# Counting the edges of each relation inside the attention instead of in the loop over edge chunks

## The reference, cut to what matters

```python
# layer 0: weighted sum over the edges
support = xn @ W
out = segment_sum(support[src] * edge_weight[:, None], dst, 625)
# layer 1: for each relation r the mean over the edges of that type
for r in range(8):
    mask = (edge_type == r)
    sums = segment_sum(xn[src] * mask[:, None], dst, n)
    cnt = segment_sum(mask, dst, n)
    out = out + (sums / max(cnt, 1)[:, None]) @ weight[r]
# layer 1 also: 16-head linear attention (exp features of 256 columns), added to x
```

## Time and profile before

| | us |
|---|---|
| median of 3 runs | 3110.17 (3106.64 to 3110.68) |
| the profiled execution | 3112.09 |
| its span in the trace | 3110.1 |
| PE busy | 2754.4 (89%) |
| DVE busy | 1789.7 (58%) |
| ACT busy | 1330.7 (43%) |
| POOL busy | 289.2 (9%) |
| mean granted TensorE clock | 0.948 of 2.4 GHz |

### The profile page before, as it was taken

One profiled execution on the slowest core, in us unless ns is written; L12 is line 12 of the kernel. 1 busy time (PEld: TensorE's weight loads), 2 busy tenths in 40 slices (PEclk: granted clock), 3 DMA queues, 4 the chain that ended last, 5 costly groups with the idle time before them and its releaser, 6 DMA issues.

```text
span 3110.1 us, 39323 instructions
## 1 busy us (share of the span) xinstructions
PE 2754.4 (89%) x16055; PEld 2433.4 (78%) x16055; DVE 1789.7 (58%) x2040; ACT 1330.7 (43%) x1761; POOL 289.2 (9%) x278
## 2 busy tenths in 40 slices
PE   3684666898999999999997599989999999999988
PEld 3674556687777777777765499978999999999987
DVE  5455883445788778877886355553344444444443
ACT  1324663224676676666772366641322222112221
POOL 3774331010000000000001000000000000000000
PEclk7796888999999999999998699999999999999999
DMA  4232003136899999999996411114222221123211
GB/s 132 56 88 61 1 1 82 63 89 237 313 327 329 316 328 329 329 321 335 324 331 176 158 36 42 42 50 133 84 65 59 65 65 59 55 80 109 75 59 67
DMA packets 129110, 456.59 MB, mean 147 GB/s; under 512 B 20503, under 2 KB 33175, under 8 KB 127795
## 3 DMA queue, kind: packets, MB, share of 16 engines
q1 hardware_dynamic: 98698, 389.85, 36.3%
q0 software_dynamic: 14512, 30.02, 4.3%
q10 hardware_dynamic: 15722, 34.22, 3.1%
HBM read 416.43 MB, written 37.49 MB: 146 GB/s over the span
## 4 chain that ended last, share of the span: by engine, by line
PE 69%; DVE 9%; DMA 7%; issue 5%; POOL 4%; ACT 3%; DVEq 1%; another core or an unknown queue 1%; ACTq 0%; SPq 0%; POOLq 0%
PE ps L188 68%; POOL scr_edges L908 4%; DMA er<-in_wd 3%; DVE es_l L213 2%; DMA wr<-in_root 1%; ACT es_h L640 1%; DMA scr_adj<-Aall 1%; DVE Aw L201 1%; DVE x L201 1%; DVE od L205 1%; DMA wr<-in_Wq 1%; DVE T_l L213 1%; POOL ws_l L213 1%; DVE st L729 1%
## 5 line engine op out<-in xcount | busy, mean ns | idle before, releaser
L213 DVE TENSOR_TENSOR es_l<-er,es_h 128x1408 fp32r<-128x1408 f32 (+1 forms) x455 | 653.1, 1445 | 192.1 <-ACT es_h L640 188.7
L640 ACT ACTIVATE es_h<-er 128x1408 fp32r<-128x1408 f32 (+1 forms) x455 | 563.4, 1242 | 270.1 <-PE ps L188 197.6
L640 ACT ACTIVATE ws_h<-wr 128x1024 fp32r<-128x1024 f32 (+1 forms) x181 | 190.9, 1056 | 591.3 <-PE ps L188 544.0
L188 PE MATMUL ps<-T_h,ws_h 128*128 128x314 f32 x1856 | 425.0, 310 | 18.3 <-DVE ws_l L213 13.4
L188 PE MATMUL ps<-T_h,ws_l 128*128 128x314 f32 x1856 | 422.2, 309 | 0.0
L188 PE MATMUL ps<-T_l,ws_h 128*128 128x314 f32 x1856 | 421.2, 309 | 0.0
L188 PEld LDWEIGHTS ps<-T_h,ws_h 128*128 128x128 f32 x1856 | 313.2, 191 | 21.4 <-issue 14.7
L213 DVE TENSOR_TENSOR ws_l<-wr,ws_h 128x1024 fp32r<-128x1024 f32 x165 | 200.4, 1216 | 200.1 <-ACT ws_h L640 197.5
L188 PEld LDWEIGHTS ps<-T_l,ws_h 128*128 128x128 f32 x1856 | 312.9, 191 | 0.0
L188 PEld LDWEIGHTS ps<-T_h,ws_l 128*128 128x128 f32 x1856 | 312.8, 191 | 0.0
L188 PE MATMUL ps<-es_h,xe_h 128*98 128x512 f32 (+1 forms) x768 | 207.9, 379 | 10.1 <-DVE es_l L213 7.1
(11 more groups left out here) (382 smaller groups left out, 5139.7 us busy)
## 6 DMA issues: line engine op xcount, KB each, us to landing
er<-in_wg SPq DMA_DIRECT2D x128, 704.0 KB, 6.7
er<-in_wu SPq DMA_DIRECT2D x128, 704.0 KB, 6.1
er<-in_wd SPq DMA_DIRECT2D x176, 512.0 KB, 5.0
wr<-in_rel SPq DMA_DIRECT2D x64, 512.0 KB
wr<-in_Wqkv SPq DMA_DIRECT2D x24, 512.0 KB
wr<-in_gate SPq DMA_DIRECT2D x16, 512.0 KB
wr<-in_w SPq DMA_DIRECT2D x14, 512.0 KB
scr_ei<-zrow ACTq DMA_DIRECT2D x1, 6272.0 KB, 30.1
```

The lines of the kernel that those rows point to most:

```text
L188: return e.matmul(out, l, r, start=start, stop=stop, skip_group_check=True)
L213: return e.tensor_tensor(lo, src, hi.bitcast(F32), ALU.subtract)
L640: q.e.activation(c.hi, c.at, ACT.Copy).then_inc(*self.s("high").up(c.key))
```

## The change

- The counts leave the loop over chunks, with the uint16 evictions, `Aall`, its three memsets and its store. The loop makes only the weights.
- The counts are made in the attention, and are there called tallies. `d_x` keeps x in memory meanwhile, since the tallies' buffers lie in x's place; x comes back after them.
- For each chunk POOL makes a one-hot `blc` (bf16), ACT makes `bod` = sign(n - target - 0.5) (bf16, "steps"), PE multiplies them (two matmuls of 314 columns), DVE adds the running sum of the bucket (`scalar_tensor_tensor` from PSUM into one of four `acc`), and POOL stores `acc` (0.314 MB) to the rows of its bucket by an indirect transfer, or to rows that nobody reads when the bucket goes on. Twice the counts are the differences of neighbouring columns.
- In each pair there are nine places (0 to 8) for two chunks: 0 after queries 0, 1 after the attend, 2 after projection 16+p, 3 after keys 1, 4 after the transposes, 5 after projection 9+p, 6 after queries 1, 7 after projection 1+p, 8 after values 1. The first are at place 4 of pair 0, the last at place 2 of pair 7.
- In the relations POOL loads twice the bytes for each relation (1.57 MB) and subtracts neighbouring columns (3135 elements a partition); ACT's ten copies at the start, and later five for each relation, are gone.
- `v_sort` has one instruction more before the indices and two elsewhere.

```diff
-        self.d_adj = nc.dram_tensor("scr_adj", (TP, NBK * NT), U16).ap()
+        self.d_adj = nc.dram_tensor("scr_adj", ((NBK + 1 + NCH) * TP, NT), F32).ap()
+        self.d_x = nc.dram_tensor("scr_x", (TP, T * D), F32).ap()
...
-        e.memset(m["Aall"].bitcast(I32)[0:TP, 0:5032], 0).then_inc(*self.s("zeros").up(0))
...
@@ t_adjacency
-            outs = self.t_pair(q, ("count", c))
-            for h in range(2):
-                ins = mm(e, outs[h][0:TP], lc[:, 0:TP], halves[h], True, True)
...
@@ a_adjacency
-                e.activation(two(u), ps.two(ps.group["count", c][0], slice(0, TP)), ACT.Copy).then_inc(*ps.out(("count", c)))
...
@@ v_adjacency
-                    e.reg_load(regs[G:G + n], m["off"][0:1, NCH + c:NCH + c + n])
...
-                o = m["Aall"][0:TP, bass.ds(v, NT)]
-                tt(e, o, m[f"c16{c % 2}"][0:TP, :], o, ALU.add).then_inc(*self.s("counts_added").up(c))
@@ p_adjacency
-        e.dma_start(self.d_adj, m["Aall"][0:TP, :]).then_inc(*self.landed("adjacency").up(0))
@@ a_spread, v_spread
-        q.wait_ge(self.landed("adjacency"), 0)
...
+    def tally(self, p, i):
+        n = 2 * (9 * p + i - 4)
+        return range(max(n, 0), min(n + 2, NCH))
+
+    def t_tally(self, q, p, i):
+        for c in self.tally(p, i):
+            outs = self.t_pair(q, ("tally", c))
+            q.wait_ge(self.s("chunk_sources"), c)
+            q.wait_ge(self.s("chunk_signs"), c)
+            for h in range(2):
+                ins = mm(q.e, outs[h][0:TP], m[f"blc{c % 4}"][:, 0:TP], m[f"bod{c % 4}"][:, h * H:(h + 1) * H], True, True)
+            ins.then_inc(*self.s("tallied").up(c))
+
+    def a_tally(self, q, p, i):
+        for c in self.tally(p, i + 1):
...
+            q.e.activation(m[f"bod{c % 4}"], self.iota, ACT.Sign, bias=m["bias"][:, c:c + 1]).then_inc(*self.s("chunk_signs").up(c))
+
+    def v_tally(self, q, p, i):
...
+            q.wait_ge(self.s("tallied"), c)
+            if c > 3:
+                q.wait_ge(self.landed(f"tally{c % 4}"), c - 4)
...
+                ins = stt(q.e, two(acc), two(was), m["same"][0:TP, c:c + 1], src, ALU.mult, ALU.add)
+
+    def p_attention(self, q):
+        q.wait_ge(self.s("normalized"), (2, T - 1))
+        e.dma_start(self.d_x, self.x).then_inc(*self.landed("x_kept").up(0))
...
+        for c in range(NCH + 2):
+            if c < NCH:
+                if c > 3:
+                    q.wait_ge(self.s("tallied"), c - 4)
+                e.tensor_scalar(m[f"blc{c % 4}"], self.iota[:, 0:128], seb[:, c, 0:1], None, ALU.is_equal).then_inc(*self.s("chunk_sources").up(c))
+            if c > 1:
+                c -= 2
+                q.wait_ge(*self.ps.done(("tally", c)))
...
+                e.indirect_dma_start(self.d_adj, to, m[f"acc{c % 4}"][0:TP, :], None).then_inc(*self.landed(f"tally{c % 4}").up(c))
...
+        e.dma_start(self.x, self.d_x).then_inc(*self.landed("x_back").up(0))
@@ v_attention (t_ and a_ alike; nine such lines in a pair)
             self.v_feature(q, "k", p, 0)
             self.v_feature(q, "q", p, 0)
+            self.v_tally(q, p, 0)
             if p:
                 self.v_tail(q, p - 1)
+            self.v_tally(q, p, 1)
             self.v_low(q, ("qkv", 16 + p))
+            self.v_tally(q, p, 2)
...
@@ p_relations
-            e.dma_start(m["A16"][0:TP, :], self.d_adj[:, r * T * NT:(r + 1) * T * NT]).then_inc(*self.landed("A16").up(r))
+            e.dma_start(steps, self.d_adj[r * N:(r + 1) * N, :].rearrange("(s p) n -> p s n", p=TP)).then_inc(*self.landed("steps").up(r))
+            q.wait_ge(self.landed("steps"), r)
+            if r > 1:
+                q.wait_ge(self.s("aggregated"), (("agg", r - 2), KD - 1))
+            e.tensor_tensor(rows(self.counts(r)[0:TP, :], T)[:, :, 0:NT - 1], steps[:, :, 1:NT], steps[:, :, 0:NT - 1], ALU.subtract).then_inc(*self.s("counts").up(r))
```

More of the change, by code:

```diff
@@ L249, in __init__ @@
         self.weights()
-        self.regs = [nc.alloc_register(mybir.EngineType.DVE, f"adj{i}") for i in range(16)]
+        self.regs = [nc.alloc_register(mybir.EngineType.DVE, f"adj{i}") for i in range(8)]
+        self.slots = [nc.alloc_register(mybir.EngineType.Pool, f"slot{i}") for i in range(8)]
     def memory(self, nc):
@@ L313, in memory @@
         at("st1", R2 + 13632, NBK * EC)
-        at("A16", R3, T * NT, U16)
-        at("ta0", R3 + 6304, NT)
-        at("ta1", R3 + 8832, NT)
-        at("icnt", R3 + 11360, NT)
+        at("dg", R2 + 13632, NCH + 1, F32R)
+        X = self.oX
+        for i in range(4):
+            at(f"bod{i}", X + i * 1280, NT, BF16)
+            at(f"blc{i}", X + 5120 + i * 256, 128, BF16)
+            at(f"acc{i}", X + 6144 + i * 2528, NT)
+        at("seb", X + 16256, NCH * 4)
+        at("bias", X + 18240, NCH)
+        at("same", X + 18752, NCH + 1)
+        at("bslot", X + 19264, NCH)
+        at("brows", X + 19776, NCH, I32)
+        at("steps", R3, T * NT)
+        at("icnt", R3 + 12576, NT)
         at("xn", R1, 5120)
@@ L747, in t_features @@
                     q.wait_ge(self.s("sorted"), "chunk ends")
-                    e.transpose(ps.one(b, 1, 0, NCH), m["m5"][0:NCH, 0:1], self.ident[0:NCH, 0:NCH]).then_inc(*self.s("sort_sums").up("chunks"))
+                    mm(e, ps.one(b, 128, 0, NCH + 1), m["ones"][0:NCH, :], m["dg"][0:NCH, :], True, True).then_inc(*self.s("sort_sums").up("chunks"))
                 hi, lo = self.t_chunk(q, (n, o))
```

166 lines of the change are left out of this document (103 added, 63 removed).

## The result

The changed kernel takes **3246.47 us** (median of 4 runs, 3243.02 to 3249.8) against 3109.43 for the kernel before in the same comparison: ratio **1.044** (95% interval 1.042 to 1.046). It is slower, as forecast; 3207 was predicted, and 3246 is inside the range of 3122 to 3278, 39 us above the middle. The profiled execution has a span of 3248.0 us, 137.9 above the one before.

What follows compares the result with a forecast made beforehand. DVE was taken to bound the loop over chunks, PE the attention. On the profiled 3112.1 us: -4.8 - 64 - 16.4 + 9 + 159 + 8 + 6 = +97, so 3209, as median 3207; range 3122 to 3278.

Steps and rivals of the forecast that it cites:

- (e): Attention: the tallies add PE matmuls (36 us) and waits (123 us) for banks, additions, exponentials and POOL; +159 us.
- (c): The spread after the loop: PE's 13.94 us idle for the counts' store and its slow start go; -16.4 us.
- (d): Copy of x, stored beside the norm's four stores, for whose end ACT and PE wait; +9 us.
- (a): The sort: DVE's first memset, beside which a POOL transfer took 6.10 us, goes; -4.8 us.
- (f): PE's clock in the attention: lower speed after idles of 2 to 3 us; +8 us, bounds 0 and +25.
- (b): Loop over chunks: DVE loses the counts' work and one register load; -64 us, bounds -69 and -54.
- (g): The relations: POOL's larger loads compete with root weights, ACT's first copies go; +6 us, bounds -1 and +14.
- The tallies slip in: Rival for the attention: banks return in time, only matmuls count, +36 instead of +159, no clock term; 3076 us, chance 0.12.
- POOL is the pace: Rival for the attention: POOL's stores and one-hots, slowed beside DVE, take 3.9 us a chunk; +216, 3264 us, chance 0.12.
- Half the waits: Rival for the attention: bank or one-hot ready sooner at half the places, waits 60 instead of 123; 3145 us, chance 0.1.
- The loop doesn't speed up: Rival for the loop: PE at low clock, or POOL, takes over at 1.45 us a chunk; 3234 us, inside the forecast.
- no idle PE before the spread: Sign of being right, between loop and spread: PE no longer idles there, as it did for 13.94 us.

Runs made afterwards that it cites:

- d_one_hot_ahead: The changed kernel with POOL making the one-hot of chunk c + 3, not c + 2, ahead of the store of chunk c; 3198.8 us.
- e_own_banks: b_matmuls with each tally taking the two banks handed out longest ago and leaving the ring where it was; 3096.6 us.
- l_all_in_ring: i_all with all tallies taking their banks from the ring again; 3121.3 us, ratio 1.005 to the kernel before.
- i_all: The changed kernel with tallies re-placed, named banks, one-hots three ahead, deeper buffers, j_bf16_steps' parts, later copy of x; 3075.2 us, ratio 0.9895 to before.
- a_none: The changed kernel without any tallies in the attention (counts meaningless), the copy of x and back kept; 3031.2 us.
- k_waits_alone: a_none with PE waiting at 35 places of the attention for four one-hots of POOL that nobody reads; 3204.0 us.
- j_bf16_steps: The changed kernel with bf16 sums and d_adj, two buffers for the relations' loads, and a later subtraction on POOL; 3229.2 us.
- h_doubled: The changed kernel with every tally matmul issued twice into the same banks; 3262.4 us.
- b_matmuls: The changed kernel with only the tally matmuls left on PE; signs and one-hots made once, no additions or stores; 3132.1 us.

## Why the prediction was right and where it was off

**Right**: the sign, that the waits of the tallies are the largest term, and their mechanism. The waits of (e) were laid out as 123 us; the trace has 120.9. Their places are those named: additions behind `z` and behind the features, the bank that `a_z` holds, store and one-hot in a row. d_one_hot_ahead, e_own_banks and l_all_in_ring each took one of these away, or put it back, for 52, 34 and 42 us of the stage. (c) and (d) came within about 1 us (-15.3 to the spread's end and +8.9), (a) within 2. In (d) the size is right and i_all confirms its cause, but less than half of it is the longer wait that was forecast. For (a), the row of 6.10 us shows POOL held up while the memset ran; in what mode of its ports DVE ran it, no row shows.

**The step that failed is (f), the clock**: "one such stretch on the path, half of it lost, less than 1.2 us a pair: +8, bounds 0 and +25". Busy time in the stage grew by 97.0 over a_none. 41.6 are the tally matmuls (e_own_banks), instead of 36; the other **55 are the clock**, outside my bounds. k_waits_alone shows the same from the other side: 108 us more of idle time, 59 more of busy time. I had read the earlier trace rows, half speed for some 3 us after an idle of 2.08, as a thing that happens once a pair. The pair shown has three stretches at 1.2 GHz, 14.6 us together; half of that is 7.3 us a pair instead of 1.2, an estimate from its rows, and seven such pairs would be 51 of the 55. So the three terms of the stage are 41.6 + 120.9 + 55.4 = 218, against 36 + 123 + 8 = 167.

**(b), the loop**, failed too: -84.0 for -64, outside its bounds of -69 and -54. "Half of 2.29 for one register load" was to remain; but the two loads were not alike, 0.60 us under cover and 1.86 us not, and it is the second that went. 15 x 1.15 us are 17 of the 20. That PE "falls to the lower clock more often" was wrong in its direction: fed every 1.18 us instead of every 1.57, without the pause of every eighth chunk and the idle of 2.08 us behind it, it went from 0.86 to 0.98. This miss and that of (f) have opposite signs; with (b) as forecast the time would have been some 3266, nearer to the end of the range. So part of the nearness is luck.

**(g)**: +12.8 for +6, within its bounds; that the first load is late for its bytes j_bf16_steps shows (half of them, 9.5 us less). The working was not right for all that: the second relation's load, 1.57 of the "2.4 MB more", goes out only behind the first subtraction, and the first load alone costs the 12.8, since it takes 68 us and the product waits for it and for POOL. What was missed behind it is +6.9 in the relations: I put POOL's subtraction "beside root products and later beside 56 us of projections", but it starts at the last sum, beside DVE's last `T_l`.

**The rivals**. *The tallies slip in* decides at waits under 5 us a pair; in the pair shown they are 20 (70.5 us, of which PE is busy 50.35). *POOL is the pace* was refuted by d_one_hot_ahead, though it came to within 20 us of the time, for another reason. *Half the waits* did not happen; with the tallies in other places (i_all) 27.8 us more than a_none are left, a quarter. *The loop doesn't speed up*: it did, by more than forecast.

**The signs** that I had named: no idle PE before the spread, and PE's waits put down to the engines named, came true. The loop was to take 160 to 175 us (147.5), ACT's wait to grow by some 9 (3.85), a pair to take 55 to 67 us (70.5) with PE busy 42 (50.35): these did not. Of the signs of being wrong one came true, a first count product that waits for POOL; POOL's stores stayed at 1.25 us, far under 2.2.

**Not settled**: what the rest of the 16 us in h_doubled's median is, and which waits cost clock. The sum of the waits does not tell: 55 us more of idle time, in pieces of up to 2.84 us, left the busy time of b_matmuls 2.6 above that of e_own_banks, while 59 us in k_waits_alone stand against 108 us of waits, 35 of them of 3.3 on average, and 55 in the change against 121. The pieces differ in length, and no run varied that alone.

## What to carry to other kernels

Work put into an engine's free time must also find its buffers free: here banks handed round in a ring and three engines in fixed order cost 121 us of waits for 42 us of matmuls, and naming banks, or making an operand one step ahead of a store, took much of that back without less work. Price the long waits on TensorE at more than their length: the waits of over 3 us in the pair shown were each followed by 3.4 to 6.0 us at half the clock, and over the stage 108 and 121 us more of waits cost 59 and 55 us of clock (k_waits_alone, the change), but 28 us only 4 (i_all), and the 55 of b_matmuls, none over 2.84, only 3. And before a stage that is full is given more, remove the added work in steps (none, matmuls alone, no POOL), since each step shows another wait.

## What the runs showed of the hardware that I had not expected

- Waits alone, without a changed matmul, took TensorE's granted clock from a mean of 0.99 to 0.83: 35 waits of 3.3 us on average, 1903 matmuls from 270.1 to 329.2 us. After one of 3.63 us it ran at 1.2 GHz for 5.9 us.
- Of two register loads on DVE close behind one another the first took 0.60 us and the second 1.86 us, 1.32 of them in the chain of waits once in eight chunks; a single load took 0.60, and there was no pause.
- ACT's Sign over 628 elements to bf16 takes 821 ns and needed no table load beside Exp: the traces of both kernels have 12 table loads, and none lies in the stage with the tallies.
- A one-hot of POOL took 1.94 us beside a subtraction of DVE that ran at the same time, against 0.62 alone; DVE's `T_l` took 5.45 us beside POOL's subtraction, against 0.80.
- A subtraction of 3135 elements on POOL takes 5.4 us, in bf16 as in float32, so less than the 7.3 scaled up from `ws_l`; the size of its input elements did not matter here.
